# Narrow attention: the queries and keys of the last four heads as two 64-column products in one PSUM bank

## The reference, cut to what matters

```python
q = (x @ wq).reshape(b, n, heads, dh).transpose(0, 2, 1, 3)
k = (ctx @ wk).reshape(b, j, heads, dh).transpose(0, 2, 1, 3)
v = (ctx @ wv).reshape(b, j, heads, dh).transpose(0, 2, 1, 3)
a = jax.nn.softmax(jnp.einsum('bhid,bhjd->bhij', q, k) * scale, axis=-1)
out = jnp.einsum('bhij,bhjd->bhid', a, v)
```

## Time and profile before

| | us |
|---|---|
| median of three runs | 3327.07 |
| lowest and highest | 3326.29, 3332.21 |
| the profiled execution | 3336.34 |
| its span, first to last instruction | 3334.6 |
| PE busy in the span | 3214.7 |
| VectorE busy | 1737.4 |
| ScalarE busy | 1476.5 |
| GpSimd busy | 805.1 |

### The profile page before, as it was taken

One profiled execution on the slowest core, in us unless ns is written; L12 is line 12 of the kernel. 1 busy time (PEld: TensorE's weight loads), 2 busy tenths in 40 slices (PEclk: granted clock), 3 DMA queues, 4 the chain that ended last, 5 costly groups with the idle time before them and its releaser, 6 DMA issues.

```text
span 3334.6 us, 39289 instructions
## 1 busy us (share of the span) xinstructions
PE 3214.7 (96%) x15478; PEld 1462.8 (44%) x15478; DVE 1737.4 (52%) x2568; ACT 1476.5 (44%) x1983; POOL 805.1 (24%) x620
## 2 busy tenths in 40 slices
PE   7999999999999999999999999999999999989997
PEld 3344344443434343435444344444434545643443
DVE  2645455454555555552234677777762222656664
ACT  3544444445454545441112656666652112326664
POOL 2544444454554554550000000000000000000000
PEclk9999999999999999999999999999999999989999
DMA  3000000000100000000000000000002000000000
GB/s 110 24 16 20 16 17 20 23 19 20 58 18 18 17 23 13 16 24 20 0 5 26 1 1 1 30 11 6 1 23 65 1 0 33 1 5 6 14 9 17
DMA packets 37284, 62.32 MB, mean 19 GB/s; under 512 B 7024, under 2 KB 24944, under 8 KB 36208
## 3 DMA queue, kind: packets, MB, share of 16 engines
q1 hardware_dynamic: 37104, 59.82, 5.9%
HBM read 57.19 MB, written 2.62 MB: 18 GB/s over the span
## 4 chain that ended last, share of the span: by engine, by line
PE 89%; DVE 5%; ACT 4%; issue 1%; POOL 0%; DMA 0%; ACTq 0%; DVEq 0%; POOLq 0%
PE bank L1589 9%; PE bank L510 9%; PE bank L595 9%; PE bank L1126 7%; PE bank L737 5%; PE bank L351 5%; PE bank L673 5%; PE bank L1059 4%; PE bank L1251 3%; PE bank L676 3%; PE bank L709 3%; PE bank L1276 3%; PE bank L1179 2%; PE bank L533 2%; DVE heads L1084 2%; PE bank L1594 2%
## 5 line engine op out<-in xcount | busy, mean ns | idle before, releaser
L1084 DVE TENSOR_REDUCE heads<-bank 128x1 f32<-128x512 f32 x960 | 598.3, 683 | 237.2 <-PE bank L1072 236.4
L544 DVE TENSOR_REDUCE heads<-bank 128x2 f32<-128x1024 f32 x320 | 392.4, 1226 | 594.7 <-PE bank L533 594.7
L581 POOL TENSOR_TENSOR heads<-heads,probs 128x1024 f32<-128x1024 f32 x160 | 389.5, 2434 | 12.5
L567 ACT ACTIVATE probs<-bank 128x1024 f32<-128x1024 f32 x320 | 328.0, 1025 | 130.3 <-PE bank L519 130.0
L577 POOL TENSOR_TENSOR heads<-probs 128x1024 f32<-128x1024 f32 x80 | 190.7, 2384 | 712.8 <-ACT probs L567 712.8
L510 PE MATMUL bank<-heads 64*128 64x512 f32 x1280 | 335.7, 602 | 0.1
L1059 PE MATMUL bank<-heads 32*128 32x512 f32 x1920 | 296.8, 628 | 25.8 <-ACT weights L1097 10.9
L595 PE MATMUL bank<-probs,values 128*64 128x512 f32 x1280 | 294.0, 601 | 1.4 <-ACT nmT L558 1.0
L1589 PE MATMUL bank<-hT,weights 128*128 128x512 f32 x640 | 291.8, 606 | 1.5 <-issue 1.5
L1097 ACT ACTIVATE weights<-bank 128x1024 f32<-128x1024 f32 x236 | 228.8, 1022 | 96.0 <-PE bank L1059 93.9
L1652 ACT ACTIVATE ctx_in<-bank,b_col 128x512 f32<-128x512 f32 x80 | 55.1, 688 | 419.4 <-PE bank L1594 323.8
(11 more groups left out here) (205 smaller groups left out, 4868.9 us busy)
## 6 DMA issues: line engine op xcount, KB each, us to landing
heads<-in_wqk SPq DMA_DIRECT2D x40, 320.0 KB, 2.8
heads<-in_wqk SPq DMA_DIRECT2D x40, 256.0 KB, 2.6
weights<-in_L_xattn_w_ff SPq DMA_DIRECT2D x3, 1600.0 KB, 7.2
weights<-in_L_xattn_ff_w SPq DMA_DIRECT2D x3, 1600.0 KB, 7.1
ctx_in<-in_ctx SPq DMA_DIRECT2D x12, 384.0 KB, 3.7
weights<-in_L_xattn_qkv_q SPq DMA_DIRECT2D x2, 1632.0 KB, 7.4
weights<-in_L_xattn_wo SPq DMA_DIRECT2D x2, 1600.0 KB, 12.2
x_res<-in_x SPq DMA_DIRECT2D x4, 640.0 KB, 13.3
```

Of the source, the lines that this page charges most:

```text
L544: nc.vector.tensor_reduce(v["negm"][:, U % 2, qb, :].rearrange("p (g k) -> p g k", g=2)[:, :, 0], M.ROWS[:, :, :], AX.X, ALU.max, negate=T ...
L567: nc.scalar.activation(v["probs"][:, kb, :, :], M.COLS[kb % 2][:, :, :], ACT.Exp, scale=float(r.work[n][0].prm["dh"]) ** -0.5).then_inc(r. ...
L581: nc.gpsimd.tensor_tensor(ps, ps, pr[:, k, :, :], ALU.add).then_inc(r.sem("part"), 1)
L1084: nc.vector.tensor_reduce(v["negm"][:, tile, qb, 32 * h + at:32 * h + at + 1], r.bank_of(item, m)[:, :], AX.X, ALU.max, negate=True).then_ ...
```

## The change

Q2 and K2 are replaced by one item, QK2, in step 0: the 64 weight columns of the queries go to partitions 0 to 63 of a bank and those of the keys to partitions 64 to 127, chunk by chunk in turn. The copy out is now four masked activations over 64 partitions each (low and high half of the query tile, low and high half of the key tile) in place of two over 128. V3 moves from step 0 to step 2, where K2 was. The waits that named K2 as the last reader of the inputs and weights (the input copy of the next batch, the weight loads on the sync engine) name V3 now. A round has one item less in the turn of banks.

```diff
                 if i == 0 and now:
-                    items += [("Q2", n), ("V3", n)]
+                    items += [("QK2", n)]
...
                 if i == 2 and now:
-                    items += [("K2", n)]
+                    items += [("V3", n)]
...
             if c == 0:
-                r.wait_full(act, "K2", n - 1)
+                r.wait_full(act, "V3", n - 1)
...
-            r.wait_out(pool, f"Q{c}", n)
+            r.wait_out(pool, f"Q{c}" if c < 2 else "QK2", n)
...
-            r.wait_out(pool, f"K{c}", n)
+            r.wait_out(pool, f"K{c}" if c < 2 else "QK2", n)
...
+        def QK_pe4(pe, r, n):
+
+            s, v, bank = r.work[n][0], n_view(r, n), r.bank_of("QK2", n)
+            r.wait_free(pe, "QK2", n)
+            for e in range(3):
+                for home, name, x, ch in ((bank[0:64, :], "wq", M.hT, CH3), (bank[64:P, :], "wk", kvT(s), keys(s))):
+                    if e < len(ch):
+                        last = nc.tensor.matmul(home, v[name][0:ch[e][1], e, 256:320], x[0:ch[e][1], e, :], start=e == 0, stop=e == len(ch) - 1)
+            last.then_inc(r.full("QK2", n), 1)
+
+        def QK_act4(act, r, n):
+
+            v, bank = n_view(r, n), r.bank_of("QK2", n)
+            r.wait(act, "cols", 20 * n)
+            r.wait(act, "q_cast", 5 * n)
+            r.wait(act, "k_cast", 5 * n)
+            r.wait_full(act, "QK2", n)
+            low, high = slice(0, 64), slice(64, P)
+            for out, part, scale, bias in ((v["QT"], low, 0, 6), (v["KT"], high, 0, 3)):
+                nc.scalar.activation(out[low, 4, :], bank[part, :], ACT.Identity, bias=M.mask[part, bias:bias + 1], scale=M.mask[part, scale:scale + 1])
+            nc.scalar.activation(v["QT"][high, 4, :], bank[low, :], ACT.Identity, bias=M.mask[low, 6:7], scale=M.mask[low, 1:2])
+            nc.scalar.activation(v["KT"][high, 4, :], bank[high, :], ACT.Identity, bias=M.mask[high, 4:5], scale=M.mask[high, 1:2]).then_inc(r.free("QK2", n), 1)
...
                 if i == 0 and now:
-                    Q_pe4(pe, r, n, 2)
-                    V_pe4(pe, r, n, 3)
+                    QK_pe4(pe, r, n)
...
                 elif i == 2 and now:
-                    K_pe4(pe, r, n, 2)
+                    V_pe4(pe, r, n, 3)
...
                 if i == 0 and now:
-                    Q_act4(act, r, n, 2)
-                    V_act4(act, r, n, 3)
+                    QK_act4(act, r, n)
...
                 if i == 2 and now:
-                    K_act4(act, r, n, 2)
+                    V_act4(act, r, n, 3)
...
-                    r.wait_full(sp, "K2", n - 1)
+                    r.wait_full(sp, "V3", n - 1)
                     load_weights(sp, s)
...
-                r.wait_full(sp, "K2", r.N - 1)
+                r.wait_full(sp, "V3", r.N - 1)
                 ff_load_first(sp, r.then)
```

More of the change, by code:

```diff
@@ L1258, in Q_act4 @@
             r.wait_full(act, item, n)
-            for u, which in ((2 * c, 0), (2 * c + 1, 1)) if c < 2 else ((4, 2),):
+            for u, which in ((2 * c, 0), (2 * c + 1, 1)):
                 last = nc.scalar.activation(v["QT"][:, u, :], r.bank_of(item, n)[:, :], ACT.Identity, bias=M.mask[:, 6:7],
```

## The result

| | median, us | runs | against the kernel before |
|---|---|---|---|
| before | 3329.64 (3326.29 to 3336.91) | 4 | |
| after | 3354.27 (3353.21 to 3355.16) | 4 | 1.0071 [1.0052, 1.0090] |
| after, once more | 3353.86 (3348.81 to 3355.38) | 5 | 1.0055 [1.0043, 1.0068], before 3334.33 in 17 runs |

The change made the kernel slower by 18 to 25 us. The prediction had said slower by 10.7 (3337.8, range 3325 to 3346): the side is right, the size is too small and the time lies outside the range. The second comparison is the better one: the kernel before was run 17 times in it, and its median was 4.7 us above that of the four runs. By it the change costs 18.3 us. The two profiled executions give 16.0: a span of 3350.6 against 3334.6.

What follows compares the result with a forecast made beforehand. PE was taken as the bound, busy 3214.7 of 3334.6 us. Waiting for copies less V3's gain gave +2.2 us and clock falls +8.5, together +10.7: median from 3327.07 to 3337.8 us, range 3325 to 3346.

Steps and rivals of the forecast that it cites:

- Part 1: QK2's products on PE: halves run side by side, 2.68 us in all, saving K2's whole PE work, 24.1 us.
- third rival: QK2's two halves run one after the other on PE, for 3362 us in all; chance 0.06.
- Part 2: ScalarE's masked copies of QK2: four take 0.78 + 3 x 0.67 = 2.79 us, ends 1.4 and 3.12.
- second rival: The four copies are as quick as two, 1.4 us, so the kernel takes 3311 us; chance 0.10.
- Part 3: Step 1's fourth row waits for all four copies; the mix starts 0.97 us later in cross rounds, 0.43 in self.
- Part 4: V3 in place of K2 in step 2: 0.97 us less in self rounds, 0.65 less in cross.
- sum of a round: Net of wait and V3's move: -0.54 us per self round, +0.54 per cross round, +2.2 us over twelve rounds.
- The clock: Behind step 1's new holes PE's clock halves in about 5 of twelve rounds, 1.7 us each: +8.5 us.
- two of five gaps: Share of similar gaps in the earlier trace followed by a clock fall, giving 12 x 0.4, about 5 falls.
- first rival: The stall in step 1 comes but the clock holds: +2.2 us, 3329.3, no change; chance 0.32.
- The base: Median of the kernel before, taken as 3327.07 us, to which the forecast change was added.
- PE's busy time: In the profile after, PE was to be busy some 20 us less in the span.

Runs made afterwards that it cites:

- run 17: Not a label but a count: the kernel before, unchanged, was run 17 times beside e5 to e8, with a median of 3334.33 us.
- e3: The changed kernel with two f32 products that nobody reads put into the hole of step 1 ahead of the fourth row: 3342.93 us, 1.0026 of before.
- e5: The changed kernel, unaltered, timed once more beside other kernels: 3353.86 us, 1.0055 of before.
- e9: The changed kernel with step 1's last row behind the mix and the key copies on VectorE behind three row maxima: 3315.12 us, 0.9954 of before.
- e11: The changed kernel with its four copies ordered query low, key high, query high, key low: 3356.83 us in one execution.
- e1: The changed kernel with the last row product of step 1 issued behind the mix instead of ahead of it: 3322.59 us, 0.9966 of before.
- e7: The changed kernel with the two key copies on VectorE, the two query copies on ScalarE, and no wait between them: 3325.43 us, 0.9974 of before.
- e8: The changed kernel with step 1's last row behind the mix and the key copies on VectorE ahead of step 1's maxima: 3328.80 us, 0.9984 of before.
- e6: The changed kernel with both query copies made first, then both key copies: 3351.09 us, 1.0049 of before.
- e10: The changed kernel with V3 left in step 0 behind QK2 instead of moved to step 2: 3342.16 us, 1.0028 of before.

## Why the prediction was right or wrong

**Part 1, right.** QK2 took 2.73 us in both kinds of round, for 2.68 predicted. The third rival fell.

**Part 2, the first step that failed.** "A further one adds 0.67" was taken from two copies over 128 partitions; a further one over 64 adds 0.78. Four take 3.13 us, not 2.79: the upper end of 3.12 that the part gave was the true value. That a copy's time doesn't go with its partitions was right, and the second rival fell.

**Part 3, right but for that term.** The fourth row of step 1 waited for all four copies, with a hole of 2.04 us for 1.9. In the cross round the mix starts 6.42 us behind the start of QK2, before 5.13 (2180.17 less 2175.04, in the round before that of the earlier trace rows): 1.29 later, and 0.97 + 0.34 = 1.31.

**Part 4 and the sum of a round.** With the 0.34 of Part 2 the sums would be 0.54 + 0.34 = +0.88 in a cross round and -0.54 + 0.34 = -0.20 in a self one. The rounds of the filled kernel, where no clock falls, show +0.91 (87.84 less 86.93, and 85.89 less 84.98), and -0.19, -0.07 and -0.18. So that one term is nearly all that was wrong in the steady rounds. Twelve of them, the first ones taken like the others: 8 x 0.91 - 4 x 0.15 = +6.7 us where +2.2 was said. The span of e3 (3341.3) is 6.7 above that of before, and its comparison gives +8.7. That the first two agree to 0.1 is luck: from the start to the second round e3 is only 0.3 us later, and behind the last QK2 2.3 us later, where the clock is at half for 6.8 us and in the kernel before for 3.4.

**The clock, right in kind and nearly in size.** Six falls came for five, at 1.55 to 1.64 us each by the table for 1.7: 6 x 1.6 = 9.6 us for 8.5; e3 beside e5 gives 9.7. What the sum had from "two of five gaps" was lucky, though: e5 shows the same six rounds hit again. The trace of before also has four more such gaps at the end of run r3 (1.53, 1.56, 2.05 and 2.12 us, up to 2514.23) that the prediction didn't count, with the clock at 0.50 behind the last two. The first rival (the clock holds) fell. By the rule of the Trainium skill ("TensorE: Matmul & The Clock Gate", section "HAM oscillation — how this bites in real kernels"), gaps shorter than the one it names would have cost nothing; six of the ten gaps of 2.04 to 2.32 us in the steady rounds were followed by a fall here, so in this kernel the measurement decides against it.

**The base.** The sum stood on a median of 3327.07 from three runs; later sets of 10 to 26 gave 3333 to 3334. Of the 16.5 us between 3337.8 and 3354.3 some 7 are this, about 4.5 the copies with what follows from them, and 1 the sixth fall. The rest, 3 to 4 us, is not settled: in the profiled executions 6.7 + 9.6 = 16.3 stand beside a measured 16.0, in part by luck, since the start and the first rounds of the runs give less than this sum and the end of the last run 2.4 us more; and the comparisons' intervals reach 4 and 6 us to either side. The kernel before spreads with its clock: of the ten runs beside e9 to e11 the two at 0.991 took 3329.03 and 3329.06 us, the one at 0.988 took 3336.97. The prediction should have used its own profiled execution, 3336.34, as a second opinion on where the kernel's median lies. So the steps that failed are two terms of the sum: the base, 3327.07 for some 3334, and the copies of Part 2, 2.79 us for 3.13. The mechanism, a hole behind the copies and a clock that falls behind some of the holes, was right.

**PE's busy time.** The prediction had PE busy for some 20 us less and it was 8.5. It put the falls into the time and left them out of the busy time, where the slow products count double.

**What wasn't foreseen: the remedies.** The sum treated the wait as what the change costs. e1 and e9 show that it is what its place in PE's order costs: 24 us of work were really saved, and with the mix ahead of the waiting row 11 of them reach the time (e1), with the copies shared as well 15 (e9), a difference that the intervals don't settle. The Trainium skill ("TensorEngine Tiling (Array Packing)", section "PSUM Bottleneck") says that array tiling quickens TensorE but not the copies out of PSUM, and advises to use ScalarE and VectorE both; here the trace agrees, with 3.13 us of copies behind 2.73 us of products, and e7, in which both engines copy, is 0.8% faster than after.

## What to carry to other kernels

When two products are laid side by side in one bank, PE's time for them can halve, but each half needs its own copies, and the bank is free only after the last of them: find the instruction that takes the next turn of that bank, and put independent work ahead of it, before counting PE's saving. Count copies by the duration of the very shape, since four half-height ones took 3.13 us where two whole-height ones take 1.45. A new hole in PE can cost more than its own length: behind six of ten holes of 2 us here, slow products cost 1.6 us more. When copies go to another engine, see what they are put in front of there, as e8 did not. And when a time comes out as forecast, check the rounds: e6 and e10 landed near their theory's number without its mechanism.

## What the runs showed of the hardware

- ScalarE's copies of 512 columns over 64 partitions follow each other at 0.78 us, in three orders of the halves; over 128 partitions the second follows at 0.67. Half the height was thus not only no quicker, but slower by 0.11 us for each one after the first.
- The granted clock fell from 2.4 to 1.2 GHz for 3.3 to 3.4 us behind six of ten holes (nine of 2.04 us, one of 2.32), in the same rounds in four profiled executions (after, e5, e6, e11). With 1.98 us of f32 products in the hole it stayed at 1.00 through all the steady rounds, and the kernel ran about 11 us sooner (3342.93 against 3353.86).
- f32 products of 64 columns with different moving operands and heights (108 and 96 rows) ran side by side almost without loss: ten records of 64 columns in 2.73 us, where six of 128 take 2.68.
